# Two chained cross-attention layers with a mixture of experts: which rows the last pass projects when, where the bias product stands, and where the second half's query transfers stand in the DMA queue

## The chip, the cores and the metric

The kernel runs on one core of a Trainium2 chip. The metric is the device time of one execution in microseconds (us), the median of several runs. The engines run side by side and meet only at semaphores: PE (TensorE) multiplies matrices, DVE (VectorE) reduces and adds, ACT (ScalarE) evaluates exponentials and empties accumulation banks, POOL (GpSimd) does elementwise work in SBUF, and SP (SyncE) starts the transfers.

## The reference

Inputs are `x` (8 batches, 56 rows, 128 channels) and a context of 8 x 1500 x 128. All is float32. Cut to what is computed:

```python
# layer 0
q = ln(x);  x = x + mha(q, q)                # self-attention, 16 heads of 8
x = x + mha(ln(x), ln(context))              # cross-attention over 1500 rows
h = ln(x);  logits = h @ rw.T + rb           # 8 experts, the best 2 gated
x = x + sum(gate * (gelu(h @ fc1.T + b1) @ fc2.T + b2))
# layer 1, weights rounded to -1, 0, 1 times their mean size
q = ln(x) @ Wq.T + bq;  k = context @ Wk.T + bk;  v = context @ Wv.T + bv
x = x + softmax(q @ k.T / sqrt(8)) @ v @ Wo.T + bo
```

where `mha` too ends with an out-projection `out @ out_w.T + out_b`.

## The kernel before

**Rows and units.** The 448 rows of x (8 batches of 56) lie in SBUF as four tiles of 112 rows (`TT`, `TP`); a tile holds two batches, and half of x is two tiles (`HT`). Each of the two cross-attentions is a pass over eight units (`B`), one for each batch; the code calls them `Unit(s, None, c)` with pass s and unit c. A unit has 12 steps k (`STEPS`), and `window(n)` on each engine writes out its work in that order. The text writes (c, k) for step k of unit c.

**A step on PE.** `scores(n, k)` multiplies keys by queries into a bank of ST (8 matmuls), ACT's `exp_step` turns it into weights, and in even steps `values` multiplies the weights of the two steps before into PO. Scores k wait for exp k-2, values k for exp k. Between these, PE runs the maxima of the next unit, one unit ahead: `max_tile(n, j)`, 24 of them, each 112 x 500 into SM and reduced by DVE (`reduce_tile`, line 883). The last unit of a pass has no maxima to make. The other products all use one bank, MI, one after the other: keys of the unit after next in steps 0 to 2, values of the next in 4 to 6, `output_back` of the previous unit in 7. Each gives back the semaphore that tells when MI has been read, `prev`, and the next one waits for it in `misc_free`. The attention result of a unit is transposed back in its successor's step 11 (`output_forth`) and put by ACT into `attnT` (`evac_on`, which counts `ont_evac`).

**Out-projections.** `project_out(n, done, prev)` waits for `done` and then makes for each row tile a product with `attnT` and a product of a row of ones with the bias, added up in the bank (lines 1234 and 1235; in float32 each product is two matmuls in the trace). DVE adds the bank to x in `add_projection`. n = 0 is the self-attention (four tiles, bank PO), 1 and 2 the halves of the first pass, 3 and 4 those of the last. Number 3 stands in (5, 10) and waits for the first four units; number 4 stands behind the last unit and does tiles 2 and 3. SP stores the halves as `x_added` reaches 4 and 5.

**Queries of the last pass.** The first half is made during the MoE. The second half (tiles 2 and 3, batches 4 to 7) is made inside the pass: `token_stats(5)` (0, 9), a power on POOL, `token_normalise(5)` (0, 11), transposes into MI and `token_gain(5)` (1, 3), the query product (1, 9), and `split_q(2, ...)` into three bfloat16 parts, (1, 10), (1, 11), (2, 0). `load_qall(2)` on SP then copies the parts by six transfers (line 393) into `qall`, one part after the other as they get ready.

**The SP queue.** It is strictly in order. For each unit n of the last pass it has: `place(n+1, 1)` (two transfers of queries, line 428, behind the scores of step 11 of unit n-1), `restack(n+1, 1)` (six transfers of 187.5 KB that lay the split keys out for the pairs of heads 4 to 7, line 412), `place(n+2, 0)` and `restack(n+2, 0)` (the same for pairs 0 to 3, behind the scores of step 5 of unit n), the load of xT for unit n+3, and in unit 1 then `load_qall(2)`. Maximum 12 of a unit is the first one that needs `restack(.., 1)`; it runs in step 4 of the unit before.

## Time and profile before

| | us |
|---|---|
| median of 3 runs | 576.57 (574.94 to 583.17) |
| the profiled execution, time | 574.07 |
| the profiled execution, span | 572.3 |
| PE busy | 514.1 (90%) |
| PE weight loads busy | 386.4 (68%) |
| DVE busy | 390.0 (68%) |
| ACT busy | 334.4 (58%) |
| POOL busy | 221.3 (39%) |

The span is the time from the first to the last instruction in the trace; the execution's own time is 1.8 us longer. Matmuls are pipelined, so a busy PE is not PE at its peak. All times are counted from the start of the span.

### The profile page before, as it was taken

Reading aid. Unit: us, or ns where it says so; the run is one execution under the profiler, and the core shown is the slowest. Engines: PE = TensorE matmul, PEld = TensorE weight load, DVE = VectorE, ACT = ScalarE, POOL = GpSimd, SP = SyncE. Lnnn points to the kernel's source line nnn. Section 1 sums busy time; section 2 is a strip of 40 time slices with the busy share of each in tenths; the row PEclk is TensorE's granted clock in tenths of the full one; section 3 lists DMA queues with packets and bytes.
Section 4 is the critical chain, followed back from the end, with each engine's and each line's share of the span. In section 5 each row is a group of like instructions: output and inputs, shape, how many; then the busy total and the mean of one; then the engine's idle time right before and its main releaser. Section 6 shows DMA issues by size and latency. Waiting matters only on the chain.

```text
span 572.3 us, 16262 instructions
## 1 busy us (share of the span) xinstructions
PE 514.1 (90%) x6648; PEld 386.4 (68%) x6648; DVE 390.0 (68%) x976; ACT 334.4 (58%) x527; POOL 221.3 (39%) x217
## 2 busy tenths in 40 slices
PE   3599748889999999999989999999998999999996
PEld 2588515466767767676767998877666676766774
DVE  5666378788887888787741434887867777786730
ACT  1166223557676777776576444376666667675573
POOL 3659744475777768423160200031404033140000
PEclk9799677899999999999999999999999999999998
DMA  5110552634354554555638401006354835535200
GB/s 160 48 55 3 143 122 50 169 89 132 95 139 112 143 145 101 137 120 143 182 73 223 141 2 31 2 1 154 72 150 113 201 92 140 144 85 121 56 4 9
DMA packets 37869, 58.69 MB, mean 103 GB/s; under 512 B 17956, under 2 KB 21404, under 8 KB 37796
## 3 DMA queue, kind: packets, MB, share of 16 engines
q1 hardware_dynamic: 37476, 57.60, 39.8%
q8 instruction: 53, 0.87, 0.6%
q14 instruction: 20, 0.16, 0.1%
q10 hardware_dynamic: 320, 0.06, 0.1%
HBM read 17.81 MB, written 0.23 MB: 32 GB/s over the span
## 4 chain that ended last, share of the span: by engine, by line
PE 68%; DVE 17%; POOL 4%; DMA 3%; issue 3%; ACT 2%; SPq 2%; DVEq 0%; ACTq 0%; POOLq 0%
PE PO L1386 14%; PE SM L1371 14%; DVE mxp L883 11%; PE ST L1343 10%; PE MI L1292 8%; PE ST L1564 4%; PE ST L1554 4%; PE MI L1282 3%; PE MI L1271 2%; POOL cxs L518 2%; PE MI L1318 2%; DMA xT<-in_ctxT 1%; ACT pts L671 1%; PE SM L1477 1%; SPq L393 1%
## 5 line engine op out<-in xcount | busy, mean ns | idle before, releaser
L883 DVE TENSOR_REDUCE mxp<-SM 112x1 f32<-112x500 f32 x374 | 241.0, 673 | 74.4 <-PE SM L1371 73.2
L671 ACT ACTIVATE pts<-ST 128x896 f32<-128x896 f32 x192 | 171.7, 913 | 31.3 <-PE ST L1343 30.8
L1371 PE MATMUL SM<-kst,qst 96*112 96x500 bf16 x374 | 142.2, 399 | 13.0 <-DVE mxp L883 9.0
L527 POOL TENSOR_TENSOR kr<-kf,ksplit 128x500 f32<-128x500 f32 x48 | 55.1, 1150 | 172.4 <-ACT ksplit L636 172.4
L1343 PEld LDWEIGHTS ST<-qst,kst 98*128 98x128 bf16 x1536 | 95.8, 100 | 29.5 <-issue 4.7
L1343 PE MATMUL ST<-qst,kst 98*128 98x112 bf16 x1536 | 106.9, 213 | 2.6 <-DMA qst<-mrow 2.6
L1386 PE MATMUL PO<-pts,vaug 125*32 125x112 f32 x3072 | 97.3, 263 | 2.3 <-ACT pts L671 1.9
L1371 PEld LDWEIGHTS SM<-kst,qst 96*112 96x112 bf16 x374 | 45.6, 129 | 61.5 <-DVE mxp L883 45.0
L1386 PEld LDWEIGHTS PO<-pts,vaug 125*32 125x32 f32 x3072 | 69.3, 109 | 14.8 <-ACT pts L671 5.7
L518 POOL TENSOR_SCALAR cxs<-cxs,cmv,crstd 125x128 f32<-125x128 f32 x84 | 67.4, 819 | 0.0
L532 POOL TENSOR_TENSOR ksplit<-kr,ksplit 128x500 bf16<-128x500 f32 x48 | 54.4, 1135 | 16.9 <-DVE ksplit L878 16.9
L648 ACT ACTIVATE vaug<-MI 125x512 f32<-125x512 f32 x48 | 28.7, 598 | 53.1 <-PE MI L1292 53.1
L1292 PEld LDWEIGHTS MI<-watt,xT 128*125 128x125 f32 x384 | 50.6, 193 | 4.1 <-ACT vaug L648 1.4
L1292 PE MATMUL MI<-watt,xT 128*125 128x128 f32 x384 | 52.4, 281 | 1.1 <-DVE hT L827 0.8
L635 ACT ACTIVATE kf<-MI,vec 128x500 f32<-128x500 f32 x46 | 31.2, 678 | 36.0 <-PE MI L1282 35.7
L1282 PE MATMUL MI<-xT,watt 128*128 128x500 f32 x92 | 48.1, 604 | 1.5 <-ACT ksplit L636 0.8
L769 ACT ACTIVATE moe<-ST,vec 128x224 f32<-128x224 f32 x64 | 28.5, 448 | 34.8 <-PE ST L1554 33.9
L878 DVE CAST ksplit<-kr 128x500 bf16<-128x500 f32 x48 | 35.0, 729 | 10.2 <-POOL kr L527 10.1
L636 ACT ACTIVATE ksplit<-MI,vec 128x500 bf16<-128x500 f32 x46 | 30.8, 670 | 0.0
L623 ACT ACTIVATE xT<-MI,vec 128x500 f32<-128x500 f32 x24 | 18.4, 767 | 16.5 <-PE MI L1271 16.4
L506 POOL TENSOR_TENSOR xrstd<-xvar,half_neg 112x2 f32<-112x2 f32 (+1 forms) x6 | 4.9, 811 | 59.5 <-DVE xvar L809 59.5
L511 POOL TENSOR_TENSOR crstd<-cvar,half_neg 125x12 f32<-125x12 f32 x8 | 18.3, 2289 | 18.0 <-DVE cvar L865 18.0
(156 smaller groups left out, 539.8 us busy)
## 6 DMA issues: line engine op xcount, KB each, us to landing
kst<-ksplit SPq DMA_DIRECT2D x192, 187.5 KB, 3.6
cxs<-in_ctx SPq DMA_DIRECT2D x8, 750.0 KB
xT<-in_ctxT SPq DMA_DIRECT2D x8, 750.0 KB, 6.5
qst<-qall SPq DMA_DIRECT2D x56, 21.0 KB, 1.9
watt<-in_watt SPq DMA_DIRECT2D x1, 768.0 KB, 5.5
cxs<-in_w1T SPq DMA_DIRECT2D x3, 256.0 KB, 5.7
cxs<-in_w2T SPq DMA_DIRECT2D x3, 256.0 KB, 6.3
pts<-in_w1T SPq DMA_DIRECT2D x3, 256.0 KB, 5.4
```

What stands on the lines that cost most here:

```text
L518: last = nc.gpsimd.tensor_scalar(cx[n.par][:, c], cx[n.par][:, c], cmv[n.par][:, c, 0:1], crstd[n.par][:, c:c + 1], ALU.subtract, ALU.mult)
L527: nc.gpsimd.tensor_tensor(kr[:, c], kf[:, c], ksplit[n.par][:, 0, c], ALU.subtract).then_inc(kr_done, 1)
L532: nc.gpsimd.tensor_tensor(ksplit[n.par][:, 2, c], kr[:, c], ksplit[n.par][:, 1, c], ALU.subtract).then_inc(k3_done, 1)
L635: nc.scalar.activation(kf[:, c], bank[:, 0:THIRD], ACT.Identity, bias=bias_k(n.s + 1)).then_inc(k_evac, 1)
L671: nc.scalar.activation(PT[:, k % PTB], ST[:, k % 2, :, 0:4 * PC], ACT.Exp, scale=SCALE).then_inc(exp_done, 1)
L878: nc.vector.tensor_copy(ksplit[n.par][:, 1, c], kr[:, c]).then_inc(k2_done, 1)
L883: nc.vector.tensor_reduce(mxp[:, j // 3, j % 3:j % 3 + 1], tile_bank(j, banks), AX.X, ALU.max).then_inc(sm_red, 1)
L1282: mm(bank[:, 0:THIRD], watt[:, n.s + 1, 1], xT[n.par][:, THIRD * i:THIRD * (i + 1)], start=True, stop=True).then_inc(kp_full, 1)
L1292: last = mm(MI[0:KC, D * c:D * (c + 1)], xT[n.par][:, at:at + KC], watt[:, n.s + 1, 2], start=True, stop=True)
L1343: last = mm(ST[:, k % 2, cc, PC * p:PC * (p + 1)], kst[n.par][:, 4 * half + p, at:at + 128], qst[n.par][:, 4 * half + p], start=True, stop ...
L1371: mm(tile_bank(j, banks), qst[n.par][0:SROWS, j // 3], kst[n.par][0:SROWS, j // 3, at:at + THIRD], start=True, stop=True).then_inc(sm_full, 1)
L1386: last = mm(PO[32 * p:32 * p + 32, PC * half:PC * (half + 1)], vaug[n.par][:, c, at:at + 32], PT[0:KC, k % PTB, cc, PC * p:PC * (p + 1)], ...
```

## The change

Three things are moved; no product leaves the kernel.

1. The out-projections of the last pass are cut differently (`OUT_PARTS`): number 3 is tiles 0 and 1 and stands in (7, 3), number 4 is tile 2, in (7, 10), behind units 4 and 5, and number 5 is tile 3 alone, at the end. They use the banks MI, MI and PO. DVE adds in (7, 5), (7, 11) and at the end, and the result is stored by three transfers.
2. In every out-projection the bias product comes first and the product with attnT second. The first bias product stands in front of the wait for attnT (but behind `misc_free`).
3. The second half's queries: statistics in (0, 4), normalisation in (0, 9), transposes (0, 10), gain (0, 11), query product (1, 10), split in (1, 11), (2, 0), (2, 1); SP runs `load_qall(2)` in unit 2 behind `restack(3, 1)` instead of at the end of unit 1, ahead of `place(3, 1)`.

```diff
-LN5_AT, Q2_AT = (1, 3), (1, 9)
-SPLIT2_AT = ((1, 10), (1, 11), (2, 0))
+LN5_AT, Q2_AT = (0, 10), (1, 10)
+SPLIT2_AT = ((1, 11), (2, 0), (2, 1))
...
+OUT_PARTS = (range(TT), range(0, HT), range(HT, TT), range(0, HT), range(HT, HT + 1), range(HT + 1, TT))
+OUT_LAYER = (0, 1, 1, 2, 2, 2)
+OUT_MISC = (1, 3, 4)
...
+                if n.s == 1 and n.c == 2:
+                    load_qall(2)
                 if n.s == 0 and (n + 4).exists():
                     load_ctx(n + 4)
...
-                if n.s == 1 and n.c == 1:
-                    load_qall(2)
...
-            for h in range(2):
-                sp.wait_ge(x_added, 4 + h)
-                sp.dma_start(rows_out[:, HT * h:HT * (h + 1)], xt[:, HT * h:HT * (h + 1)]).then_inc(stored, 16)
-            sp.wait_ge(stored, 32)
+            for n in range(3, 6):
+                sp.wait_ge(x_added, n + 1)
+                ts = OUT_PARTS[n]
+                sp.dma_start(rows_out[:, ts[0]:ts[-1] + 1], xt[:, ts[0]:ts[-1] + 1]).then_inc(stored, 16)
+            sp.wait_ge(stored, 48)
...
+                    if n.s == 1 and (n.c, k) == (0, 4):
+                        token_stats(5)
                     if n.s == 1 and (n.c, k) == (0, 9):
-                        token_stats(5)
+                        token_normalise(5)
                     if n.s == 1 and (n.c, k) == (0, 11):
-                        token_normalise(5)
-                    if n.s == 1 and (n.c, k) == LN5_AT:
                         token_gain(5)
...
-                    if n.s == 1 and (n.c, k) == OUT_AT:
+                    if n.s == 1 and (n.c, k) == (7, 5):
                         add_projection(3)
+                    if n.s == 1 and (n.c, k) == (7, 11):
+                        add_projection(4)
...
-                pe.wait_ge(*done)
-                layer = (n + 1) // 2
-                ts = range(TT) if n == 0 else range(HT * ((n - 1) % 2), HT * ((n - 1) % 2 + 1))
-                bank = MI if n in (1, 3) else PO
-                for i, t in enumerate(ts):
+                layer = OUT_LAYER[n]
+                bank = MI if n in OUT_MISC else PO
+                for i, t in enumerate(OUT_PARTS[n]):
                     tile = bank[0:TP, D * i:D * (i + 1)]
-                    mm(tile, attnT[:, TP * t:TP * (t + 1)], watt[:, layer, 3], start=True, stop=False)
-                    last = mm(tile, ones_row[:], rows[0:1, D * layer:D * (layer + 1)], start=False, stop=True)
+                    mm(tile, ones_row[:], rows[0:1, D * layer:D * (layer + 1)], start=True, stop=False)
+                    if i == 0:
+                        pe.wait_ge(*done)
+                    last = mm(tile, attnT[:, TP * t:TP * (t + 1)], watt[:, layer, 3], start=False, stop=True)
...
-                    if n.s == 1 and (n.c, k) == OUT_AT:
+                    if n.s == 1 and (n.c, k) == (7, 3):
                         prev = project_out(3, (ont_evac, B + B // 2), prev)
+                    if n.s == 1 and (n.c, k) == (7, 10):
+                        prev = project_out(4, (ont_evac, B + B - 2), prev)
...
-            project_out(4, (ont_evac, 2 * B))
+            project_out(5, (ont_evac, 2 * B))
```

## Rows read from the trace of the kernel before

**Rows 1.** The profile's chain of work that ended last: shares of the span by engine.

```profile
PE 68%; DVE 17%; POOL 4%; DMA 3%; issue 3%; ACT 2%; SPq 2%; DVEq 0%; ACTq 0%; POOLq 0%
```

**Rows 2.** Timeline, SP queue, last pass: start us, length us, queue, line, transfer, count.

```profile
387.17 1.24 SPq L428 DMA_DIRECT2D qst<-qall  x2
...
412.95 1.27 SPq L428 DMA_DIRECT2D qst<-qall  x2
...
425.77 4.48 SPq L393 DMA_DIRECT2D qall<-qsplit  x6
...
431.84 4.24 SPq L412 DMA_DIRECT2D kst<-ksplit  x6
...
440.11 1.27 SPq L428 DMA_DIRECT2D qst<-qall  x2
...
463.99 1.26 SPq L428 DMA_DIRECT2D qst<-qall  x2
...
488.13 1.27 SPq L428 DMA_DIRECT2D qst<-qall  x2
```

**Rows 3.** Timeline, PE, units 1 and 2; in brackets the idle time before and its releaser.

```profile
400.33 1.08 PE L1282 MATMUL MI<-xT,watt 128*128 128x500 f32 x2 [0.70 <-DMA xT<-in_ctxT]
...
408.11 0.41 PE L1211 MATMUL MI<-ident,xn 112*128 112x112 f32 x2 [0.52 <-ACT ksplit L636]
...
411.18 1.14 PE L1292 MATMUL MI<-watt,xT 128*125 128x128 f32 x8 [0.80 <-DVE hT L827]
...
421.48 0.65 PE L1221 MATMUL MI<-hT,watt 128*128 128x224 f32 x2 [0.63 <-DVE on L918]
...
439.25 0.39 PE L1371 MATMUL SM<-kst,qst 96*112 96x500 bf16 x1 [1.68 <-issue]
```

**Rows 4.** DMA issues by line: count, KB each, median us to landing.

```profile
kst<-ksplit SPq DMA_DIRECT2D x192, 187.5 KB, 3.6
...
qall<-qsplit SPq DMA_DIRECT2D x12, 56.0 KB, 2.1
...
out_x<-xt SPq DMA_DIRECT2D x2, 112.0 KB, 2.7
```

**Rows 5.** Timeline, DVE, units 0 and 2 of the last pass.

```profile
390.35 0.68 DVE L883 TENSOR_REDUCE mxp<-SM 112x1 f32<-112x500 f32 x1 [0.96 <-PE SM L1371]
...
395.48 0.47 DVE L802 BATCH_NORM_STATS2 xstat<-xt 112x6 f32<-112x128 f32 x2
...
429.29 0.38 DVE L848 TENSOR_TENSOR qsplit<-qr,qsplit 128x224 bf16<-128x224 f32 x1
...
432.59 1.95 DVE L883 TENSOR_REDUCE mxp<-SM 112x1 f32<-112x500 f32 x3 [0.64 <-PE SM L1371]
```

**Rows 6.** Timeline, unit 5 (step 10) and unit 7 of the last pass.

```profile
523.24 0.47 PE L1235 MATMUL MI<-rows,ones_row 1*112 1x128 f32 x2
...
524.09 0.68 DVE L883 TENSOR_REDUCE mxp<-SM 112x1 f32<-112x500 f32 x1 [1.09 <-PE SM L1371]
...
554.03 0.35 PEld L1386 LDWEIGHTS PO<-pts,vaug 125*32 125x32 f32 x16 [0.33 <-ACT pts L671]
```

**Rows 7.** Stretches: us, then busy and count of PE, PEld, DVE, ACT, POOL; PEclk.

```profile
550.00:563.00 13.00, 12.24 (x283) 9.20 (x275) 0.57 (x3) 10.30 (x15) 0.00 (x0) 1.00 0.02 4
...
566.10:567.30 1.20, 0.74 (x4) 0.40 (x3) 0.00 (x0) 0.31 (x1) 0.00 (x0) 0.77 0.00 0
```

**Rows 8.** Timeline, PE, the end of the kernel.

```profile
565.77 0.42 PE L1331 MATMUL ST<-ident,on 56*128 56x56 f32 x2 [0.66 <-DVE on L918]
...
566.65 0.70 PE L1234 MATMUL PO<-watt,attnT 128*112 128x128 f32 x2 [0.46 <-ACT attnT L683]
...
568.67 0.76 PE L1235 MATMUL PO<-rows,ones_row 1*112 1x128 f32 x2
```

**Rows 9.** The first projection in the timeline; all projection additions: ns min/median/max, times, forms.

```profile
65.45 0.74 PE L1234 MATMUL PO<-watt,attnT 128*112 128x128 f32 x2 [0.49 <-ACT attnT L740]
...
L930 DVE TENSOR_TENSOR xt<-xt,PO x3: 422/422/687, 71.1 to 569.5; 112x256 f32<-112x256 f32 x2, 112x512 f32<-112x512 f32 x1
```

More of the change, by code:

```diff
@@ L926, in add_projection @@
                 dve.wait_ge(op_full, n + 1)
-                t = slice(0, TT) if n == 0 else slice(HT * ((n - 1) % 2), HT * ((n - 1) % 2 + 1))
-                width = D * (t.stop - t.start)
-                bank = MI if n in (1, 3) else PO
-                nc.vector.tensor_tensor(xt[:, t], xt[:, t], bank[0:TP, 0:width].rearrange("p (t d) -> p t d", d=D),
+                ts = OUT_PARTS[n]
+                t = slice(ts[0], ts[-1] + 1)
+                bank = MI if n in OUT_MISC else PO
+                nc.vector.tensor_tensor(xt[:, t], xt[:, t],
+                                        bank[0:TP, 0:D * len(ts)].rearrange("p (t d) -> p t d", d=D),
                                         ALU.add).then_inc(x_added, 1)
@@ L1192, in _ @@
             normalise_unit(Unit(1, None, B - 1))
-            add_projection(4)
+            add_projection(5)
         @block.tensor
@@ L1227, in project_out @@
                 misc_free(prev)
[L1228 to L1232 removed]
+                layer = OUT_LAYER[n]
+                bank = MI if n in OUT_MISC else PO
+                for i, t in enumerate(OUT_PARTS[n]):
                     tile = bank[0:TP, D * i:D * (i + 1)]
[L1234 to L1235 removed]
+                    mm(tile, ones_row[:], rows[0:1, D * layer:D * (layer + 1)], start=True, stop=False)
+                    if i == 0:
+                        pe.wait_ge(*done)
+                    last = mm(tile, attnT[:, TP * t:TP * (t + 1)], watt[:, layer, 3], start=False, stop=True)
                 last.then_inc(op_full, 1)
```

1 line of the change is left out of this document (removed).

## Prediction

> **What bounds the kernel now.** I read the chain of work that ended last first: PE holds 68% of it and DVE 17% [rows 1]. So a microsecond counts when PE does not have it. Next I read the SP queue in order of time. Its place transfers (L428) wait for fixed scores of each unit, and so they mark the units of the last pass: from the middle of one unit to the middle of the next it is 25.78 us (387.17 to 412.95), 27.16 (to 440.11), 23.88 (to 463.99) and 24.14 (to 488.13) [rows 2]. The stretch in which the second half's queries are made, the first two, is thus 4.9 us longer (52.94) than twice the mean of the two that follow (48.02). The waits in front of PE's instructions say where it goes: 0.70 for an xT transfer at 400.33, 0.52 and 0.80 on both sides of the token transposes at 408.11, 0.63 ahead of the query product at 421.48, and 1.68 before the maximum matmul at 439.25 [rows 3]. The last one is put down to "issue", that is, to nothing the profile shows. In the code that matmul, the 13th of unit 3, waits for `kst_loaded[1]`; and the restack transfers behind this semaphore were issued until 431.84 + 4.24 = 436.08 [rows 2], with a median landing of 3.6 us [rows 4]. So it is the restack. Last I read the end instruction by instruction: from 565.77 on nothing but one chain runs: a transpose, ACT's copy, four product pairs, an addition, an output transfer [rows 8].
>
> **The query part.** *The restack.* At the end of unit 1 SP issues six qall transfers for 4.48 us from 425.77, and only then place and the six restack transfers of unit 3's second half [rows 2]. The change puts qall behind them. They then land 4.5 us earlier, at about 435.2 instead of 439.7, and PE, which is ready at 439.25 - 1.68 = 437.57, finds them there 2.4 us ahead: the 1.68 goes whole. The qall issues then end where the restack's did, at 436.1, and SP has nothing to do until 440.11 less the 1.7 saved, so they fit; landed at about 438.2 (2.1 us [rows 4]), they are just ahead of place(4,0), whose data is first used in the next unit. Nothing on PE is late next.
>
> *The transposes*, (1,3) to (0,10). They leave the place between key and value products, where MI goes from product to product: 0.41 of PE and the waits of 0.52 and 0.80, 1.73 in all [rows 3]. At (0,10) MI has been free since step 6, and the 0.41 comes to lie in front of the 0.70 wait for xT at 400.33, whose transfer SP releases and not PE: hidden, and 0.41 dear if the transfer came sooner. The statistics move to (0,4), where DVE waits 0.96 for PE per reduction; the two themselves take 0.47, with aggregates and addition I estimate twice that [rows 5]. One step's idle time covers it; cost nothing, 0.9 without cover. POOL's power follows its key parts as before.
>
> *The query product*, (1,9) to (1,10): its wait of 0.63 for DVE goes, its 0.65 stays [rows 3].
>
> *The split* moves by one step. DVE gets one subtraction (0.38, L848) and the cast more in the first two steps of unit 2, where its reductions are close to the chain. One step offers 0.64 of idle time [rows 5]. I take 0.3 us of loss; bounds 0 (all in idle time) and 0.7 (both in the chain).
>
> The sum: of the 4.9 excess 0.70 (xT), 0.65 (product) and 0.3 (split) stay, so 3.3 us are saved. Bounds: 1.0, if the stall alone goes and the split costs 0.7; 3.9 at the other end.
>
> The row shows 4.48 us for six issues and 2.1 us for one landing. The Trainium skill ("DMA: Bandwidth & Descriptors", Issuing engines are not separate DMA queues) says that the time a sequencer takes to start a DMA is usually small beside the DMA. By that rule the order on SP would matter little, the stall would be transfer time and stay, and the whole sum below would be 3.9 us instead of 5.5. That is rival B.
>
> **Unit 5.** Four product pairs (two of attnT, two of the bias) leave (5,10). The last takes 0.40 until the next matmul, PE has no gap there, and DVE waits 1.09 for the maximum matmul behind them [rows 6]. So PE is the bound and 4 x 0.40 = 1.6 us are saved; the 1.09 is also the lower bound, if DVE took over then.
>
> **Unit 7.** The same four come back at (7,3), two more at (7,10). Unit 7 has no maxima. It runs in a loop: an exp, the values that wait 0.33 for it [rows 6], the next scores, the next exp. The four at (7,3) stand between scores 3 and 4. They push the loop by 1.6 and swallow one 0.33, since exp 3 is done when its values come: +1.3. The two at (7,10) stand before scores 11, on which exp 11, the last values and the tail hang: 2 x 0.40 = +0.8. Sum +2.1. Bounds: +1.2, if more waits are swallowed; +4.2, if all six cost the 0.70 that one costs in the tail. The granted clock is 1.00 through unit 7 [rows 7], so I take 0.40. DVE and SP idle there: both additions and two output transfers cost nothing, and MI is read out by DVE long before PE asks for it.
>
> **The tail.** Before: four pairs from 566.65, the last starting at 568.67, 0.67 to 0.70 each; an addition of 0.42; a transfer [rows 8, 9]. After: one bias pair in front of the wait for attnT, one pair behind it. The bias can start when the transpose ends (565.77 + 0.42 = 566.19), and the wait ends at 566.65. At 0.40 it is hidden, at 0.70 it is 0.25 late; I take 0.1. PE saves 3 x 0.69 - 0.1 = 2.0. The addition has 128 columns: from 0.42 for 256 and 0.69 for 512 [rows 9] I get 0.29, 0.13 saved. The last transfer has 56 KB instead of 112 KB, whose landing is 2.7; 56 KB to SBUF took 2.1 [rows 4]; I take 0.2 of these 0.6. The tail saves 2.3; bounds 1.9 and 3.1.
>
> The granted clock is 0.77 from 566.1 to 567.3 [rows 7]: it falls there from 2.4 GHz to 1.2 GHz, after PE had waited 0.66 and 0.46 us [rows 8]. The Trainium skill ("TensorE: Matmul & The Clock Gate", Part 1) calls the throttled state the default and says that activity releases it. By that, a bias pair in an idle gap can only hold the clock up longer, and the tail would save some 2.6 instead of 2.3.
>
> **The first projection** (self-attention): eight pairs from 65.45, after a wait of 0.49 [rows 9]. One bias pair now fills the wait, so the chain behind (addition, layer norm, queries) starts 0.45 us sooner; bounds 0 and 0.5. The other two projections of the first pass are only reordered. The one in the MoE has waited for the same semaphore in `misc_free` already: cost nothing, gain nothing.
>
> **Sum:** -3.3 - 1.6 + 2.1 - 2.3 - 0.45 = -5.55 us. In the profiled execution's own terms (574.07 with a span of 572.3) that is 568.5, with a span of 566.8. The median of the runs, 576.57, lies 2.5 above the profiled one; less 5.55 it gives 571.0, which I predict. A median of few runs can fall anywhere between these two.
>
> **Rivals.**
> A, the forecast, 571.0: 0.72.
> B, the stall of 1.68 stays, because other traffic sets the restack's landing and not its issue. For: the profile names no releaser [rows 3]. Against: the same restack in the units that last 24 us has room. 3.9 saved, 572.7: 0.07.
> C, DVE becomes the bound where PE's waits go: maximum matmuls wait for reductions instead. The query part then gives 1.0 and unit 5 1.1, so 2.7 saved, 573.8. For: DVE holds 17% of the chain. Against: it waits 0.96 and 1.09 for PE [rows 5, 6]. 0.12.
> D, more than that: unit 7 takes the four pairs for 0.7 and the clock stays up in the tail. 7 saved, 569.5: 0.06.
> E, slower: the clock falls in unit 7. If its new pauses (for exp, before scores 4) drop it to half there, the values and scores of a pair of steps, about 1.1 us, double: six pairs +6.6, the six products +1.8, so -5.55 + 8.4 = +2.9 and 579.4. From four pairs of steps at half clock on it decides. Against it: the clock held 1.00 with a wait of 0.33 in each pair [rows 6, 7], and the change adds work there. 0.03.
>
> **How the numbers follow.** 1.0 for the query part alone gives 573.3, +4.2 for unit 7 alone 573.1, both 575.4. Downward, the profiled execution less 5.55 is 568.5 and less 7 is 567.1. So the range is 567.5 to 575.4; it leaves out E and little else. 2% is 11.5 us, about what a measurement of this kernel can tell from no change, and no case reaches it: within 2% 0.97, faster by over 2% 0.02, slower by over 2% 0.01.
>
> **What would show it.** Right: on SP, restack L412 right behind place at the end of unit 1 and qall L393 behind it; no PE wait of a microsecond in unit 2; the middles of units 0 and 2 49.6 us apart instead of 52.9; four pairs' time gone from unit 5; unit 7 2.1 longer; one product pair between the last attnT and the addition. Wrong: waits for L883 or L827 in place of those removed, a PE wait for an xT or kst transfer in unit 2 or 3, a clock below 1.00 in unit 7, or unit 7 over 3 us longer.

## The result, and the profile after

| | median us | lowest to highest | executions |
|---|---|---|---|
| before, beside the changed kernel | 578.54 | 574.94 to 583.17 | 4 |
| changed | 571.3 | 567.6 to 578.54 | 4 |
| before, later, beside the last experiments | 578.86 | 575.99 to 586.51 | 17 |
| changed, the same | 573.02 | 569.58 to 575.27 | 6 |

The changed kernel takes 0.9878 [0.9829, 0.9927] of the time before, and in the second comparison 0.9894 [0.985, 0.9937]. It is 5.8 to 7.2 us faster, 1.1 to 1.2%. (A program's slower kind of execution is left out of the ratios here and below, which are thus not the quotients of the medians.) The prediction was 571.0, 5.55 us less.

The profiled execution of the changed kernel is the longest of its four, 578.54 with a span of 576.3, and so longer than that of before (574.07, span 572.3). Total spans can't be compared here; the reason has a section of its own below. So I compare stretches that begin and end at the same instruction. A good mark is the transpose of a unit's maxima (L1308 before, L1317 after), once per step 6 ("middle") and once per step 1 of the units of the last pass. The first pass is the same in both: from its second unit on four units take 25.98 to 26.00 us each, the next one 25.70 to 25.75.

The timeline of the changed kernel, PE: the middles of units 0, 1 and 2 (start us, length us), and between the last two a maximum matmul that waits for DVE and, at 444.04, the one of unit 3 that waited 1.68 before [rows 3].

```profile
397.55 0.21 PE L1317 MATMUL ST<-identb,mparts 112*8 112x112 bf16 x1
...
421.17 0.21 PE L1317 MATMUL ST<-identb,mparts 112*8 112x112 bf16 x1
...
437.13 0.42 PE L1380 MATMUL SM<-kst,qst 96*112 96x500 bf16 x1 [0.75 <-DVE mxp L889]
...
444.04 0.38 PE L1380 MATMUL SM<-kst,qst 96*112 96x500 bf16 x1
...
446.66 0.21 PE L1317 MATMUL ST<-identb,mparts 112*8 112x112 bf16 x1
```

From the first to the last transpose it is 49.11 us; before it was 52.68 (388.98 to 441.66). By the marks of the prediction, the place transfers on SP, it is 49.15 (395.74 to 444.89), where it forecast 49.6. The wait of 1.68 is gone: the matmul that had it starts 22.9 us after the middle of unit 1 instead of 24.6, without a wait. A new wait of 0.75 for a DVE reduction stands seven maximum matmuls ahead of it. The SP queue of the same stretch, start and length:

```profile
430.10 1.27 SPq L433 DMA_DIRECT2D qst<-qall  x2
431.46 4.65 SPq L417 DMA_DIRECT2D kst<-ksplit  x6
436.15 3.98 SPq L398 DMA_DIRECT2D qall<-qsplit  x6
444.89 1.27 SPq L433 DMA_DIRECT2D qst<-qall  x2
```

Place is now first, the restack right behind it, and the six qall transfers (3.98 us of issue) fill the time up to the next place, as in [rows 2] they did not. In the chain of work that ended last little changes against [rows 1]: PE gains a point, and so does DVE.

```profile
PE 69%; DVE 18%; POOL 4%; DMA 3%; issue 3%; ACT 2%; SPq 2%; DVEq 0%; ACTq 0%; POOLq 0%
```

Unit 7 in the timeline of the changed kernel: the pairs of tiles 0 and 1 between two groups of scores (the first and the last of their four rows), the exp ahead of them and the one that they delay, and the two pairs of tile 2.

```profile
556.37 0.57 PE L1352 MATMUL ST<-qst,kst 98*128 98x112 bf16 x8
556.87 0.47 PE L1241 MATMUL MI<-rows,ones_row 1*112 1x128 f32 x2
...
556.98 0.92 ACT L677 ACTIVATE pts<-ST 128x896 f32<-128x896 f32 x1 [0.31 <-PE ST L1352]
...
558.07 0.47 PE L1244 MATMUL MI<-watt,attnT 128*112 128x128 f32 x2
558.38 0.56 PE L1352 MATMUL ST<-qst,kst 98*128 98x112 bf16 x8
...
558.97 0.92 ACT L677 ACTIVATE pts<-ST 128x896 f32<-128x896 f32 x1 [1.08 <-PE ST L1352]
...
566.40 0.47 PE L1241 MATMUL MI<-rows,ones_row 1*112 1x128 f32 x2
566.80 0.47 PE L1244 MATMUL MI<-watt,attnT 128*112 128x128 f32 x2
```

A pair takes 0.40 (556.87 to 557.26). ACT waits 1.08 for its scores, where it waited 0.31 one exp earlier. And the end of the changed kernel:

```profile
571.87 0.67 PE L1340 MATMUL ST<-ident,on 56*128 56x56 f32 x2 [0.66 <-DVE on L924]
572.47 0.76 PE L1241 MATMUL PO<-rows,ones_row 1*112 1x128 f32 x2
572.64 0.31 ACT L689 ACTIVATE attnT<-ST,vec 128x56 f32<-128x56 f32 x1 [2.34 <-PE ST L1340]
573.16 0.77 PE L1244 MATMUL PO<-watt,attnT 128*112 128x128 f32 x2
573.97 0.29 DVE L936 TENSOR_TENSOR xt<-xt,PO 112x128 f32<-112x128 f32 x1 [2.15 <-PE PO L1244]
```

The bias pair starts at 572.47, before attnT is written (572.64 + 0.31 = 572.95), and one pair is left behind it, as the prediction had it. Here the clock is already at 1.2 GHz at the transpose: it falls at 570.7, so each pair costs 0.69.

The stretches of all profiles, in us between maxima transposes ("m" the middle of a unit, "f" the one in its step 1) or to the end, and the granted clock's mean over the span:

| kernel | span | clock | m0 to m1 | m1 to m2 | m2 to m3 | m3 to m4 | m4 to m5 | m5 to f6 | f6 to m6 | f7 to end |
|---|---|---|---|---|---|---|---|---|---|---|
| before | 572.3 | 0.962 | 25.70 | 26.98 | 24.15 | 24.14 | 24.44 | 14.13 | 10.91 | 21.69 |
| changed | 576.3 | 0.945 | 23.63 | 25.48 | 24.14 | 24.61 | 24.44 | 12.59 | 10.91 | 21.76 |
| e1 | 576.9 | 0.950 | 25.02 | 25.33 | 24.14 | 27.23 | 24.44 | 14.14 | 10.91 | 21.80 |
| e2 | 578.5 | 0.952 | 23.56 | 31.09 | 24.15 | 24.14 | 24.43 | 14.14 | 10.91 | 21.31 |
| e3 | 579.5 | 0.945 | 25.02 | 26.97 | 24.16 | 24.15 | 24.44 | 12.58 | 12.46 | 20.87 |
| e4 | 570.1 | 0.956 | 23.51 | 25.49 | 24.15 | 24.14 | 24.44 | 14.19 | 10.91 | 20.63 |
| e5 | 572.0 | 0.952 | 23.50 | 25.48 | 24.14 | 24.14 | 24.43 | 12.58 | 12.42 | 22.54 |
| e6 | 569.0 | 0.965 | 23.51 | 25.47 | 24.14 | 24.14 | 24.47 | 12.58 | 12.21 | 21.82 |
| e7 | 562.5 | 0.987 | 23.51 | 25.48 | 24.14 | 24.14 | 24.44 | 12.58 | 10.91 | 20.89 |
| e8 | 574.1 | 0.954 | 24.80 | 26.15 | 24.32 | 24.14 | 24.43 | 12.59 | 12.43 | 20.87 |
| e10 | 567.8 | 0.985 | 24.26 | 25.47 | 24.15 | 24.13 | 24.43 | 12.59 | 11.17 | 20.90 |
| e11 | 573.3 | 0.945 | 23.51 | 25.48 | 24.37 | 24.14 | 24.43 | 12.58 | 14.85 | 21.57 |
| e12 | 567.4 | 0.984 | 23.57 | 25.48 | 24.14 | 24.14 | 24.43 | 14.18 | 10.92 | 19.60 |
| e13 | 578.2 | 0.972 | 25.00 | 29.60 | 24.14 | 24.14 | 24.43 | 14.13 | 12.45 | 20.61 |

The same code gives the same stretch to about 0.1 us, wherever no wait for a DMA and no fall of the clock lies in it. So one profile of a kernel settles a part of 0.5 us, which its total time does not.

### The profile page after: what moved, and what is told of

Its sections match the earlier page's. It is cut to its first block, busy times and chain, and to the rows that moved or that the text cites. A ratio compares the mean times of both kernels' runs of the same rounds, so it can differ in the third digit from the quotient of the medians.

```text
span 576.3 us, 16260 instructions
## 1 busy us (share of the span) xinstructions
PE 523.0 (91%) x6648; PEld 393.7 (68%) x6648; DVE 390.8 (68%) x977; ACT 334.6 (58%) x527; POOL 222.3 (39%) x217
## 4 chain that ended last, share of the span: by engine, by line
PE 69%; DVE 18%; POOL 4%; DMA 3%; issue 3%; ACT 2%; SPq 2%; DVEq 0%; ACTq 0%; POOLq 0%
PE PO L1395 14%; PE SM L1380 14%; DVE mxp L889 12%; PE ST L1352 10%; PE MI L1301 7%; PE ST L1575 4%; PE ST L1565 4%; PE MI L1291 3%; PE SM L1488 2%; PE MI L1280 2%; POOL cxs L524 2%; PE MI L1327 1%; DMA xT<-in_ctxT 1%; ACT pts L677 1%; SPq L398 1%
## 5 line engine op out<-in xcount | busy, mean ns | idle before, releaser
L524 POOL TENSOR_SCALAR cxs<-cxs,cmv,crstd 125x128 f32<-125x128 f32 x84 | 67.4, 817 | 0.0
L1291 PE MATMUL MI<-xT,watt 128*128 128x500 f32 x92 | 49.6, 621 | 1.4 <-ACT ksplit L642 0.8
## 6 DMA issues: line engine op xcount, KB each, us to landing
kst<-ksplit SPq DMA_DIRECT2D x192, 187.5 KB, 3.6
```

The source lines that it names most:

```text
L524: last = nc.gpsimd.tensor_scalar(cx[n.par][:, c], cx[n.par][:, c], cmv[n.par][:, c, 0:1], crstd[n.par][:, c:c + 1], ALU.subtract, ALU.mult)
L1291: mm(bank[:, 0:THIRD], watt[:, n.s + 1, 1], xT[n.par][:, THIRD * i:THIRD * (i + 1)], start=True, stop=True).then_inc(kp_full, 1)
```

## The experiments

### e1 and e2: the two halves of the query part, each alone on the kernel before

e1 changes only the order on SP; e2 only the steps of statistics, transposes, product and split.

```
# e1, in the SP window, on the kernel before
+                if n.s == 1 and n.c == 2:
+                    load_qall(2)
                 if n.s == 0 and (n + 4).exists():
...
-                if n.s == 1 and n.c == 1:
-                    load_qall(2)
# e2, on the kernel before
-LN5_AT, Q2_AT = (1, 3), (1, 9)
-SPLIT2_AT = ((1, 10), (1, 11), (2, 0))
+LN5_AT, Q2_AT = (0, 10), (1, 10)
+SPLIT2_AT = ((1, 11), (2, 0), (2, 1))
+                    (token_stats at (0, 4), token_normalise at (0, 9), token_gain at (0, 11))
```

> The kernel before with one edit: SP issues the six qall transfers of the second half in unit 2 behind the restack, not at the end of unit 1 ahead of it. Theory (issue order makes the stall): the wait of PE before the 13th maximum matmul of unit 3 (1.68 us before) is gone, and the middles of units 1 and 2 lie 25.5 us apart instead of 27.16; units 0 to 1 stay at 25.78. Rival B (other traffic sets the landing): a wait of over 1 us stays there and the distance stays near 27. Rival C (DVE takes over): the wait is gone but waits for reductions take its place, distance over 26.5.

> The kernel before with the other half of the query part: statistics, normalisation, transposes, gain, query product and split at the new steps, the qall transfers left in their old place on SP. Theory: units 0 to 1 shrink from 25.78 to 24.4 (the waits of 0.52 and 0.80 around the transposes and their 0.41 go), but the split is a step later now, so SP reaches the restack about 2 us later and the stall before the 13th maximum grows from 1.68 to about 3.5; units 1 to 2 28.3. Rival C (DVE bound): units 0 to 1 stay above 25.2. If the restack's landing does not hang on SP's order, the stall stays at 1.7.

Measured: 578.68 and 580.34 us, one execution each, beside 579.97 and 578.96 for the kernel before; the totals say nothing. The stretches do. e1, SP queue and PE in unit 2:

```profile
427.47 1.26 SPq L428 DMA_DIRECT2D qst<-qall  x2
428.83 4.62 SPq L412 DMA_DIRECT2D kst<-ksplit  x6
433.50 4.12 SPq L393 DMA_DIRECT2D qall<-qsplit  x6
...
440.46 0.38 PE L1371 MATMUL SM<-kst,qst 96*112 96x500 bf16 x1
```

With place and restack ahead of qall the wait of 1.68 is gone, and m1 to m2 goes from 26.98 to 25.33. The trace also has the landing of each transfer: before, the last of the six restack transfers landed at 439.15, and the maximum matmul that "waited for nothing visible" started at 439.25; in e1 it landed at 436.50, 4 us ahead. Rival B, that other traffic and not the order on SP holds this restack up, is refuted. Counted from m1 the restack starts 6.1 us earlier (11.1 us after m1 instead of 17.2). That is more than the 4.48 us of qall issues by which the prediction moved it: SP, being in order, had also waited for the split in front of them. The Trainium skill ("DMA: Bandwidth & Descriptors", Issuing engines are not separate DMA queues) calls the time to initiate a DMA usually small beside the DMA. Here one issue took about 0.7 us, a third to a fifth of a landing of 2.1 (qall) or 3.6 us (restack) [rows 4], and six in a row took 4.12 to 4.65 us, which is not small for what stands behind them.

e2, the same two queues:

```profile
428.22 7.28 SPq L393 DMA_DIRECT2D qall<-qsplit  x6
435.55 1.26 SPq L428 DMA_DIRECT2D qst<-qall  x2
436.91 4.27 SPq L412 DMA_DIRECT2D kst<-ksplit  x6
...
433.16 0.42 PE L1371 MATMUL SM<-kst,qst 96*112 96x500 bf16 x1 [0.75 <-DVE mxp L883]
...
444.30 0.64 PE L1371 MATMUL SM<-kst,qst 96*112 96x500 bf16 x1 [4.06 <-issue]
```

m0 to m1 goes from 25.02 (e1) to 23.56: the new steps save 1.46 there. But the qall issues, on which SP sits from 428.22, wait for a split that is now one step later and last until 435.50; the restack starts 19.7 us after m1 instead of 17.2, 2.5 us later than in [rows 2], and PE stalls 4.06, 2.4 more than before. Behind the stall the clock is at 1.2 GHz from 444.2 for 3.4 us. Together m1 to m2 is 31.09. The later split is only usable with the new order on SP: the two halves are one change.

The later split also has a price: the wait of 0.75 for the reduction, in e2 and in the changed kernel. In e1 the same matmul (15.9 us after m1 in all three) waits for nothing. The reason stands in front of the reduction on DVE. Before, then changed, then POOL in the changed kernel:

```profile
426.66 0.28 DVE L845 CAST qsplit<-qr 128x224 bf16<-128x224 f32 x1
...
435.39 1.09 DVE L851 CAST qsplit<-qr 128x224 bf16<-128x224 f32 x1
...
435.11 1.25 POOL L533 TENSOR_TENSOR kr<-kf,ksplit 128x500 f32<-128x500 f32 x1 [15.19 <-ACT ksplit L642]
```

The same cast takes 1.09 us instead of 0.28. In all ten profiles with the new steps it starts 0.3 us into an operation of POOL, ends 0.1 us after it and takes 1.09 to 1.10; in the four with the old steps (before, e1, e3, e13) POOL is idle and it takes 0.28. That POOL's work holds it up fits all fourteen, but no run moved the one without the other. Since the query product's wait of 0.63 is saved in the same stretch, changed and e1 come out alike there (25.48 and 25.33).

### e3 and e4: the query part undone, projection 3 put back

e3 is the changed kernel with steps and SP order of the queries as before. e4 is the changed kernel with projection 3 (tiles 0 and 1, four pairs) at (5, 10) again instead of (7, 3), and its addition there too.

```
# e3, on the changed kernel
-LN5_AT, Q2_AT = (0, 10), (1, 10)
-SPLIT2_AT = ((1, 11), (2, 0), (2, 1))
+LN5_AT, Q2_AT = (1, 3), (1, 9)
+SPLIT2_AT = ((1, 10), (1, 11), (2, 0))
+                    (statistics, normalise, gain and load_qall(2) where they were)
# e4, on the changed kernel
-                    if n.s == 1 and (n.c, k) == (7, 3):
+                    if n.s == 1 and (n.c, k) == (5, 10):
                         prev = project_out(3, (ont_evac, B + B // 2), prev)
```

> The changed kernel with the whole query part undone: only the new out-projections (cut in three, bias product first). Theory: the middles of units 0 to 2 52.9 us apart as before, the half unit with step (5,10) 1.6 shorter, unit 7 2.1 longer, the tail 2.3 shorter; from the middle of unit 5 to the end 58.0 instead of 59.7. Rival: unit 7 takes the four pairs for less, then under 57.5; or for 0.7 each, then over 59.5.

> The changed kernel with projection 3 (tiles 0 and 1) back in step (5,10), addition there too; projections 4 and 5 stay. Theory: unit 5 pays 1.6 more, unit 7 1.3 less, so from the middle of unit 5 to the end it is 0.3 us longer than in the changed kernel. If the loop of unit 7 has room for the four pairs, it is over 1 us longer; if the loop pays more for them than unit 5 did, it is shorter.

Measured: 581.25 and 571.94 us (one execution each). In e3 m0 to m2 is 51.99, in the changed kernel 48.99 (e11) to 49.11: the query part is worth 2.9 to 3.0. In e4 m5 to f6 is 14.19 against 12.59: moving projection 3 out of unit 5 saves 1.6. In unit 7, from its first maxima transpose to the start of the last 16 values matmuls, it is 12.79 before and in e1, 13.49 in e4, 14.79 in the changed kernel and e3. So tile 2's two pairs cost 0.70, the four at (7, 3) 1.30.

But e3 also shows what the prediction did not have: f6 to m6 is 12.46, not 10.91. The clock is at 1.2 GHz from 536.6 for 3.4 us. From m5 to the end e3 is thus only 0.8 shorter than before (57.06 against 57.88), where 1.7 was expected. This is taken up in e11.

e3's tail, where the clock is still at 2.4 GHz:

```profile
576.12 0.47 PE L1241 MATMUL PO<-rows,ones_row 1*112 1x128 f32 x2
576.29 0.31 ACT L689 ACTIVATE attnT<-ST,vec 128x56 f32<-128x56 f32 x1 [1.90 <-PE ST L1340]
576.65 0.47 PE L1244 MATMUL PO<-watt,attnT 128*112 128x128 f32 x2
577.15 0.29 DVE L936 TENSOR_TENSOR xt<-xt,PO 112x128 f32<-112x128 f32 x1 [1.45 <-PE PO L1244]
```

From attnT (576.60) to the addition it is 0.55, against 1.02 in the changed kernel at half clock.

### e5: the bias product behind attnT's again

```
-                    mm(tile, ones_row[:], rows[...], start=True, stop=False)
                     if i == 0:
                         pe.wait_ge(*done)
-                    last = mm(tile, attnT[...], watt[:, layer, 3], start=False, stop=True)
+                    mm(tile, attnT[...], watt[:, layer, 3], start=True, stop=False)
+                    last = mm(tile, ones_row[:], rows[...], start=False, stop=True)
```

> The changed kernel with the order inside the out-projections undone: the wait for attnT first, then the attnT product, then the bias product. Theory: from the end of ACT's last attnT to the addition after it 5.8 us in the first projection instead of the changed kernel's 5.26, and in the tail 1.75 at half clock or 1.2 at full, instead of 1.02 and 0.55; so 0.5 to 0.7 us in each place, 1.1 in all. Rival: a semaphore or bank hand-over sets the start of the products, then under 0.2 in each.

Measured: 573.82 us (one execution). The tail of e5:

```profile
567.83 0.31 ACT L689 ACTIVATE attnT<-ST,vec 128x56 f32<-128x56 f32 x1 [2.50 <-PE ST L1340]
568.19 0.77 PE L1243 MATMUL PO<-watt,attnT 128*112 128x128 f32 x2 [0.46 <-ACT attnT L689]
568.88 0.77 PE L1244 MATMUL PO<-rows,ones_row 1*112 1x128 f32 x2
569.68 0.29 DVE L936 TENSOR_TENSOR xt<-xt,PO 112x128 f32<-112x128 f32 x1 [2.68 <-PE PO L1244]
```

Two pairs stand behind attnT (568.14), and the addition starts 1.54 later instead of 1.02: the order of the two products is worth 0.52 in the tail. In the first projection, from the end of the last attnT to the addition, it is 5.80 in before, e1, e2 and e5 and 5.26 in the changed kernel, e3, e4 and e6: 0.54.

### e6 and e7: is the spread between executions the clock?

Executions of one kernel differ in the mean granted clock (0.945 to 0.960 in e11's six, whose times roughly follow it). In the profile of before it is at 1.2 GHz for 10.2 us from 20.6 us on, in that of the changed kernel for 27.3 us from 17.7 on. Stretches from 20 us on; us, busy and count of PE, PEld, DVE, ACT, POOL, and the granted clock. Before:

```profile
20.00:40.00 20.00, 16.46 (x146) 14.79 (x145) 13.25 (x48) 8.51 (x14) 11.24 (x6) 0.74 0.12 42
```

Changed:

```profile
20.00:40.00 20.00, 16.46 (x97) 15.21 (x96) 11.57 (x44) 5.77 (x9) 7.33 (x4) 0.50 0.07 22
40.00:60.00 20.00, 20.00 (x205) 15.75 (x205) 7.84 (x19) 10.64 (x21) 16.24 (x15) 0.87 0.05 21
```

In the same 20 us PE does 97 instead of 146 instructions. The change touches nothing before the first projection, yet the last attnT of the self-attention is ready at 65.31 before and at 72.93 in the changed kernel, 7.6 us later. To test this, e6 adds matmuls on a constant tile whose results are never read ("fillers", 128x512 bf16) in the gaps of PE's first 27 us; nothing of the computation changes.

```
+            def fill(count, bank):
+                for _ in range(count):
+                    mm(bank, warm[:, 0:128], warm[:], start=True, stop=True)
...
+            pe.wait_ge(warm_ready, 1)
+            fill(14, ST[:, 1, 1])
             pe.wait_ge(ld_x, 32)
...
+            fill(3, ST[:, 1, 1])
...
+            fill(12, ST[:, 1, 1])
             pe.wait_ge(sa_q, 1)
...
+                    fill(6, ST[:, 1, 1])     (and 8 behind, both in the second turn of the loop)
```

e7 adds more of them: at the end of the self-attention, around the first query product, ahead of the first pass and in the tail.

> The changed kernel with 43 filler matmuls (128 x 128 by 512, bfloat16, results never read) in PE's waits of the first 27 us. Theory, new: the spread between executions and up to 8 us of time is the granted clock at half during the self-attention (10 to 27 us at 0.50 there in the executions seen so far, and the last attnT of the self-attention at 65 to 73 us with it). With the fillers the clock is full from about 10 us on and stays: last attnT of the self-attention by 61 us in every execution, median 562 to 566, ratio to the kernel before 0.975. Rival: the fillers delay real work by as much as the clock gives, or the clock does not hold; then last attnT at 65 or later and the median stays at 568 or above.

> As the one with fillers at the start, and more fillers in PE's waits at the end of the self-attention, around the first query product, before the first scores and in the tail. Theory: the clock, at half for 13.7 and 10.2 us between 61 and 92 us in the kernel before, stays full: from the addition of the first projection to the first transpose of the maxima 24 us instead of 26.5, the first unit 1 us sooner, the tail at full clock from the last exp on (6.1 us instead of 7.0). Some 4 us less than with the start alone, 559 to 562. Rival: in these stretches a chain of DVE, POOL and DMA is the bound, so that PE's clock gives under 1.5 us.

e6 measured 571.03 us, 570.38 to 571.5 (4 executions), 0.9887 [0.9837, 0.9937] of before. Its stretch from 20 us on:

```profile
20.00:40.00 20.00, 16.75 (x145) 12.49 (x145) 13.02 (x48) 8.49 (x14) 11.09 (x6) 0.91 0.12 43
```

The spread is 1.1 us in four executions, where the changed kernel's was 11 and 5.7 us. That the start makes a good part of the spread is also seen without e6. In the nine profiles without fillers the last attnT of the self-attention is ready the later, the longer the clock was at 1.2 GHz from about 20 us on: at 65.3 us with 10.2 us of it (before), 66.4 and 67.4 with 13.7 (e5, e4), 68.7 and 68.9 with 17.1 (e11, e8), 69.9 and 70.0 with 20.5 (e1, e2), 72.9 and 73.1 with 27.3 (changed, e3).

The level that I expected, 562 to 566, was wrong; attnT at 66.99 and a median above 568 are the numbers of my rival, that the fillers delay real work by as much as the clock gives. The 145 instructions in the stretch hold 12 fillers, so that 133 of the kernel's own stand against 146 in before. Nor is attnT sooner in e10, e12 and e13 (66.8 to 67.5), where the clock was at 2.4 GHz from 6.0 to 6.6 us on until 60.6 or later. Whether the first ten microseconds at half clock cost nothing, because DVE and POOL bound the self-attention then, or the fillers ate what the clock gave, is open: no run had the full clock there without fillers.

e7 measured 569.2 us, 564.38 to 575 (4 executions), 0.989 [0.9795, 0.9984]. Its profiled execution (span 562.5) has the first projection in 2.96 instead of 5.26 and a tail that is 0.9 shorter. In this same execution the clock was at 1.2 GHz from 18.9 us for 10.2 us, and the fillers in that time ran at half speed (0.43 us apart instead of 0.22); it was the fastest of the four all the same. The spread is as wide as without fillers (564.38 to 575), and what the slower three had is not on record. The 2.96 did not come back either: with the same fillers there e10 and e12 have 5.26 and 5.27 and e13 5.80, the clock being at 1.2 GHz from about 61 us on. The stretch with the first queries was no shorter (26.2 us from addition to next transpose of maxima); there the rival was right.

### e8: an xT load between the restack's issues

In e8 SP issues the xT load behind the fourth of six restack transfers instead of behind all six, since the wait for xT (0.70 in [rows 3]) comes and goes.

```
                 for t in range(TERMS):
+                    if t == 4 and between is not None:
+                        load_xT(between)
                     sp.dma_start(kst[n.par][...
```

> The changed kernel with the xT load issued behind the fourth of the six restack transfers instead of behind the sixth. In executions so far PE waited between 0 and 1.8 us for xT at the start of one unit of the last pass. Theory: the load is issued 1.5 us sooner, no such wait is left, and the middles of units 0 to 5 of the last pass lie no more than 24.5 us apart but for the second step (25.5). Rival: the restack's last two transfers, now behind 750 KB, land late, and PE waits for kst at the start of a unit instead.

Measured: 575.91 us (one execution). PE in e8:

```profile
404.53 0.60 PE L1381 MATMUL SM<-kst,qst 96*112 96x500 bf16 x2 [1.26 <-issue]
...
429.72 0.60 PE L1381 MATMUL SM<-kst,qst 96*112 96x500 bf16 x2 [0.63 <-issue]
```

The rival was right: the restack is the tighter one, and the load between its issues makes PE wait 1.26 and 0.63 us for it. m0 to m2 is 50.95 instead of 48.99. It isn't the issue of the load that does it, which took SP 0.55 us. The last restack transfer, issued at 397.05 behind the load's 750 KB, landed at 404.44, 7.4 us later, where the same one in the kernel before took 4.75; the load landed at 403.19, and PE started at 404.53. Here it is other traffic that delays a restack, the mechanism of rival B, which e1 had ruled out for the stall before.

### e10 to e13: unit 6, and the changed kernel again

e11 is the changed kernel, unchanged. e10 is it with e7's fillers, more of them in two places of the self-attention (21 for 12 behind the value product, 13 for 8 in the second turn of the loop), and three fillers in each of the first three steps of unit 6. e12 is e10 without those of unit 6, with projection 3 at (5, 10). e13 is the kernel before with the fillers of e12.

```
# e10, in the window of PE
+                    if n.s == 1 and n.c == 6 and k < 3:
+                        misc_free(prev)
+                        fill(3, MI[:])
                     if k == BACK_STEP and prv.exists():
```

> The changed kernel with filler matmuls wherever PE waits long: at the start (57, more than before behind the value product of the self-attention), at the end of the self-attention, around the first query product, before the first scores, three in each of the first three steps of unit 6 of the last pass, and in the tail. Theory, new: since projection 3 left (5,10), the granted clock falls for a few us at the start of unit 6 in four of six executions, and unit 5's middle to unit 6's middle then takes 25.0 us instead of 23.5, which gives back the 1.5 saved. With the fillers there it is 23.5. Start at full clock in every execution: last attnT of the self-attention by 64.5, median 561 to 565, highest under 568. Rival: the fall at unit 6 is not due to PE's idle time, then 25.0 stays; fillers at the start cost what they give, then a median of 568 or more.

> The changed kernel itself once more, on the same chip as the others of this call, for a ratio with more executions and a second profile. Theory: query part and out part together save 5.5 us but 1.5 of them are given back where the clock falls in unit 6; ratio to the kernel before 0.990 to 0.993. In the profile either 25.0 or 23.5 from unit 5's middle to unit 6's. Rival: the first ratio, 0.988, holds because of a different start; then the two profiles' first 100 us differ by no more than their clocks explain and the ratio stays at 0.988.

> The changed kernel with projection 3 back in (5,10) and the fillers of the start, the first projection and the tail, none in unit 6. Theory: projection 3 in (5,10) keeps PE busy there, so no fall of the clock at unit 6: middle to middle 25.1, unit 7 1.2 us shorter than in the changed kernel. Against the kernel with fillers in unit 6 it loses 0.3 to 0.4 us; within 1 us of its median. Rival: if the fall comes by chance, it shows here too, 26.5.

> The kernel before with the same fillers at the start, the first projection, before the first scores and in the tail. It takes the clock's chance out of the start. Theory: 5.5 us faster than the kernel before (569 to 572 median, against 575 to 580), spread under 4 us; and 5.5 to 6 us slower than the changed kernel with its fillers (the change's own worth: query part 3.0, unit 5 1.5, unit 7 -2.0, tail 2.3 at equal clock, first projection 0.5). Rival: if fillers and change overlap (both shorten the waits of tail and first projection), the difference is 4 or less.

| | median us | lowest to highest | executions | ratio to before |
|---|---|---|---|---|
| e11, the changed kernel | 573.02 | 569.58 to 575.27 | 6 | 0.9894 [0.985, 0.9937] |
| e10 | 570.73 | 569.6 to 574.58 | 6 | 0.9869 [0.9831, 0.9906] |
| e12 | 570.47 | 569.31 to 571.43 | 4 | 0.9862 [0.9816, 0.9908] |
| e13 | 579.75 | 570.86 to 582.27 | 12 | 0.9964 [0.9912, 1.0015] |

The stretch m5 to m6 of e11, cut where its clock falls:

```profile
520.00:527.80 7.80, 6.71 (x101) 3.98 (x90) 5.83 (x13) 4.10 (x8) 0.00 (x0) 1.00 0.36 83
527.80:538.00 10.20, 9.84 (x101) 7.27 (x99) 4.53 (x8) 2.75 (x3) 0.00 (x0) 0.50 0.26 57
```

From 527.8 PE runs at 1.2 GHz for 10.2 us and takes them for 101 instructions, as many as it did in the 7.8 us before. f6 to m6 is 14.85 instead of 10.91. Without projection 3 at (5, 10) and without fillers in unit 6 the clock fell at 525 to 537 us in five of seven profiled executions (e3, e5, e6, e8, e11; not in the changed kernel's first and e7); with it there in one of six (e13; not in before, e1, e2, e4, e12). The mean of m5 to m6 is 24.90 in the first group and 25.32 in the second (25.07 without e13). So in these profiles 0.4 of the 1.54 that unit 5 gives is left on average, and unit 6 takes back 1.1. e10, with fillers there, had no fall and 23.76, in one profile.

The cause is open. Five of seven against one of six comes about once in 13 by chance alone. And what PE did right ahead of the fall was the same in all thirteen, from 4 us before f6 to 1.5 us behind it; before (no fall), then e11 (fall at 527.8):

```profile
524.52:530.02 5.50, 4.49 (x57) 2.44 (x57) 4.09 (x11) 3.23 (x6) 0.00 (x0) 1.00 0.54 122
521.74:527.24 5.50, 4.49 (x57) 2.44 (x57) 4.14 (x11) 3.23 (x6) 0.00 (x0) 1.00 0.42 97
```

From m5 to f6 PE is busy 96.0% of the time with projection 3 and 95.6% without. That the missing work brings the fall is thus a guess that the counts favour; that the fall comes or not by something else that differs between executions is not excluded.

Of the expectations of this group e12's held (m5 to m6 25.10, unit 7 1.3 shorter). e10's did not: its median of 570.73 is far from 561 to 565, and attnT was ready at 66.9 instead of 64.5. e11's ratio came out just below the 0.990 to 0.993 that I expected, its m5 to m6 at 27.43 instead of 25.0.

e13 missed its expectation, a narrow spread at the level that separates before and changed. Its PE in unit 2, and the two stretches around the stall:

```profile
443.10 0.39 PE L1378 MATMUL SM<-kst,qst 96*112 96x500 bf16 x1 [2.65 <-issue]
```

```profile
440.00:443.50 3.50, 0.85 (x10) 0.58 (x9) 1.01 (x2) 0.60 (x1) 1.27 (x2) 1.00 0.64 141
443.50:446.90 3.40, 3.40 (x24) 3.05 (x22) 1.90 (x6) 1.51 (x2) 0.00 (x0) 0.50 0.14 29
```

The stall, 1.68 in the profile of before, is 2.65 here; PE is busy 0.85 of 3.5 us, and then the clock is at 1.2 GHz for 3.4 us. m1 to m2 is 29.60, 2.6 longer than in before. The stall is longer because the six restack issues took 5.26 us here instead of 4.24. Between the medians of e13 and e12 lie 9 us, where the stretches in undisturbed form account for 4.5 (query part 3.0, unit 7 and tail 1.0, first projection 0.5). What the change removes is thus in some executions more than its waits: in e13 also the fall of the clock behind the stall, which the profile of before and e3 (a stall of 1.67) don't have. How often the kernel before has it is not on record.

e12 is the fastest median and the steadiest, but its interval overlaps with that of the changed kernel: no version was shown to beat it.

## Why the prediction was right, point by point

The mechanisms of the prediction came, but that the time is so close (571.0 against 571.3) is luck in part: the kernel before came out at 578.54 and 578.86 in larger numbers of executions, not at the 576.57 from which I subtracted, and the difference is 7.2 and 5.8, not 5.55. The base too low and the saving too small cancelled. The parts:

| part | forecast | measured | from |
|---|---|---|---|
| query part | -3.3 | -2.9 to -3.0, in the profile of before -3.6 | e3, m0 to m2 |
| unit 5 | -1.6 | -1.54 to -1.6, with 1.1 given back in unit 6 | e4, m5 to f6 |
| unit 7 | +2.1 | +2.0 (1.30 + 0.70) | f7 to the last values |
| tail | -2.3 | -1.9 at half clock, up to -2.8 | last values to the end |
| first projection | -0.45 | -0.54 | attnT to addition |

The sum in the trace, from m0 to the end, is 183.30 to 178.71 = -4.6, with a wait for xT of 0.5 in unit 4 that has nothing to do with the change. Less that, and with the first projection, it is -5.6. But the profile of before has such a wait too (0.70 in [rows 3]), which e1 and e3 don't have. With both left out it is -4.9, and what unit 6 takes back in some executions comes off that. The parts thus explain less than the 5.8 and 7.2 of the medians. Where the rest comes from is not shown; falls of the clock like the one in e13 and the spread between executions are candidates.

**Query part: mechanism right, two terms mis-sized.** The stall went by the order on SP alone (e1), whole, as forecast; rival B is out. Its margin was larger than forecast, 4 us (e1) instead of 2.4, since SP had waited for the split as well. The step "I take 0.3 us of loss" for the split failed: it costs 0.75, just over my upper bound of 0.7. The subtraction and a cast lie in front of a reduction on which a maximum matmul waits, and the cast takes 1.09 us there instead of 0.28, with POOL at work beside it. That wait for a reduction is rival C's sign, in small. The idle 0.64 of [rows 5] was measured at another step and was no cover. The second term is the xT wait of 0.70. I held it for a fixed part of the stretch that stays; e1 and e3 don't have it (25.02 instead of 25.70), in the changed kernel 0.5 of it appears in unit 4, and e1 has 1.81 at the same place (and behind it, from 481.8, 3.4 us at 1.2 GHz, so that m3 to m4 is 27.23):

```profile
480.29 1.08 PE L1282 MATMUL MI<-xT,watt 128*128 128x500 f32 x2 [1.81 <-DMA xT<-in_ctxT]
```

It is a wait that comes and goes with the landing of the load, and one profile of before can't tell that. Since the transposes were to be hidden in it, their 0.41 was not tested as such; the stretch m0 to m1 shrank by 1.5 where it is absent. The sum itself had a slip: the waits and work that it names in the two stretches (0.70, 1.73, 0.63, 0.65, 1.68) add up to 5.4, not to the 4.9 of excess, and what goes by them is 4.04 less 0.3 = 3.7, not 3.3. Its upper bound of 3.9 has no working.

**Unit 5: right, but not to its end.** PE was the bound and the 1.6 came. Rival C (DVE as bound) is refuted here: e4 against the changed kernel gives the full 1.6. What failed is the silent assumption that the gain is kept. Rival E had the mechanism, a fall of the clock where PE waits more, but put it in unit 7, where the change adds work, and the clock held there in every profile. It came in unit 6, behind the place from which work was taken, and cost 1.3 to 3.9 us in the profiles that had it. Whether the move brought it is not shown (e11). I had looked for the price of a move only at its new place.

**Unit 7: right.** Tile 2's pairs 0.70 (0.8 forecast), the four at (7, 3) 1.30 (1.3). The swallowed wait for the exp is real: four pairs of 0.40 push the loop by 1.3. Moving projection 3 is worth 0.3 in itself, and less than nothing when the clock falls in unit 6: e4 and e12, which leave it at (5, 10), are no slower than the changed kernel.

**Tail: right within its bounds, and the clock sets which.** From the start of the last 16 values matmuls to the end it is 8.89 before, 9.01 in e1; 6.98 in the changed kernel, 7.15 in e4, 6.08 in e3. From attnT to the addition the changed kernel saves 1.86 (2.88 to 1.02; 1.97 forecast), and the output transfer lands in 1.56 instead of 1.95 us (0.39; 0.2 forecast). But the clock fell 1.4 us after the start of those matmuls and not 3.4, which makes attnT 0.45 later. At half clock the bias pair is not hidden (572.47 + 0.69 = 573.16, 0.2 behind attnT; 0.25 forecast), with 2.4 GHz it is. The Trainium skill ("TensorE: Matmul & The Clock Gate", Part 1) says that activity releases the throttle, from which I had the bias pair hold the clock up. The traces don't test it: in the changed kernel and in e4 the clock had fallen before that pair started (at 570.7 and 564.1), in e3 it held until 577.6, behind it.

**First projection: right**, 0.54 for 0.45, because the pair is at half clock there (0.70 a pair) and the wait covers most of it.

**What the prediction didn't see** is the size of what differs between executions: 8 to 11 us before and 6 to 11 in the changed kernel, as much as the change is worth and more, of which the clock in the first 45 us makes up to 8 (attnT at 65.3 to 73.1). I took the profiled execution's distance from the median (2.5) as an offset. That the profile of the changed kernel is 4 us longer than that of before, while from m0 on it is 4.6 us shorter, shows how little a single span says here.

## What to carry to other kernels

On a queue that issues strided transfers in groups, a group costs what stands behind it its issue time (4.0 to 5.5 us per six) and the wait for its own data: put the group that somebody waits for first and the one with slack behind it. Where the profile names no releaser for a stall, look for a transfer that landed just before its end, then whether it was issued late (before) or landed late behind other traffic (e8). Compare kernels between like instructions inside their profiles, since total spans may differ more by the clock of the start than by the change. When a step of work moves on DVE, look at what POOL does at its new place. When work is taken out of a stretch where PE waits in turn for another engine, read the next unit, and the clock in it, before counting the gain.

## What the runs showed of the hardware that I had not expected

- The length of the time at 1.2 GHz near the start varies from one execution to the next with the same instructions: it starts at 17.5 to 20.6 us and lasts 10.2 to 27.3 us in the profiles without fillers. The last attnT of the self-attention is ready at 65.3 us with the shortest and at 73.1 with the longest.
- With matmuls whose results nobody reads it was mostly gone (e6: 3.4 us at half clock at 34.2, spread 1.1 us in four executions; none before 60 us in e10, e12 and e13), yet not reliably: in e7 the clock fell between them at 18.9, and they took 0.43 us each instead of 0.22.
- A stall of PE of 4.06 us (e2), 2.65 us (e13) or 1.81 us (e1) was followed by 3.4 us at 1.2 GHz, one of 1.68 us (before) or 1.67 us (e3) was not.
- A cast of 128x224 on DVE took 0.28 us in the four profiles where POOL was idle beside it, and 1.09 us in the ten where it started inside an operation of POOL; it ended 0.1 us after that.
- In e8 the last restack transfer (187.5 KB), issued behind a load of 750 KB, landed 7.4 and 7.7 us after its issue; without a load ahead of it, in the kernel before, it took 3.9 and 4.75.
- In e10 and e12 the stretch from the last maxima transpose of the first pass to the first one of the last pass (in step 1 of its first unit) took 90.2 and 90.1 us, in e13 91.4 (with 3.4 us at 1.2 GHz in it), in the others 88.8 to 89.5. Why is open.
